# Third LayerNorm of a decoder layer: normalised by ScalarE in two passes instead of by VectorE in one

## The reference, cut to what matters

```
def _layernorm(x, axis=-1, eps=1e-05):
    m = jnp.mean(x, axis=axis, keepdims=True)
    v = jnp.var(x, axis=axis, keepdims=True)
    return (x - m) / jnp.sqrt(v + eps)
...
x = _layernorm(x + attention(x))      # 16 heads, causal, top-32 keys of each row kept
x = _layernorm(x + experts(x, ...))   # 8 experts 256 -> 512 -> 256, relu, gated sum
x = _layernorm(x + ffn(x))            # Hadamard, 4-bit activations, ternary weight
return x
```

## Time and profile before

| | |
|---|---|
| time, median of 3 runs | 606.18 us (605.2 to 607.4) |
| time of the profiled execution | 605.08 us |
| its span, first to last instruction | 603.3 us |
| busy share of the span: PE, PEld | 87%, 75% |
| busy share: DVE, ACT, POOL | 78%, 64%, 57% |
| third LayerNorm on DVE (line 841, out_sb) | 16 instructions, 9.9 us busy in all |

### The profile page before, as it was taken

One profiled execution on the slowest core, in us unless ns is written; L12 is line 12 of the kernel. 1 busy time (PEld: TensorE's weight loads), 2 busy tenths in 40 slices (PEclk: granted clock), 3 DMA queues, 4 the chain that ended last, 5 costly groups with the idle time before them and its releaser, 6 DMA issues. The chain is left out here.

```text
span 603.3 us, 22386 instructions
## 1 busy us (share of the span) xinstructions
PE 527.5 (87%) x8180; PEld 450.2 (75%) x8180; DVE 472.6 (78%) x2995; ACT 385.9 (64%) x909; POOL 344.5 (57%) x336
## 2 busy tenths in 40 slices
PE   4567459999899999998999989998999999989941
PEld 3455347888778878887888878887888888878830
DVE  1777996968988998698899998999899999633213
ACT  2787765866667667675677657776686767555520
POOL 3447661875566646555375646665656556656831
PEclk9799767999999999999999999999999999999985
DMA  7253341010000010000100100010001000000000
GB/s 217 80 184 131 109 145 37 14 37 20 3 21 20 3 54 21 2 3 3 54 20 3 56 3 20 3 55 2 20 3 38 3 3 2 20 0 3 19 0 17
DMA packets 21933, 21.85 MB, mean 36 GB/s; under 512 B 1856, under 2 KB 19776, under 8 KB 21824
## 3 DMA queue, kind: packets, MB, share of 16 engines
q1 hardware_dynamic: 21824, 20.42, 10.8%
HBM read 18.32 MB, written 2.10 MB: 34 GB/s over the span
## 5 line engine op out<-in xcount | busy, mean ns | idle before, releaser
L478 POOL TENSOR_TENSOR h_lo<-h_raw,h_hi 128x512 f16<-128x512 f32 x128 | 148.7, 1164 | 126.8 <-ACT h_raw L598 125.8
L792 PE MATMUL ps_o<-w_hi,h_lo 128*128 128x256 f16 x512 | 139.8, 273 | 4.7 <-POOL h_lo L478 4.5
L776 PE MATMUL ps_z<-x1t_hi,w_lo 128*128 128x256 f16 x512 | 140.4, 274 | 0.7 <-DVE x1t_lo L934 0.7
L776 PE MATMUL ps_z<-x1t_lo,w_hi 128*128 128x256 f16 x512 | 140.2, 274 | 0.0
L776 PE MATMUL ps_z<-x1t_hi,w_hi 128*128 128x256 f16 x512 | 140.1, 274 | 0.0
L792 PE MATMUL ps_o<-w_lo,h_hi 128*128 128x256 f16 x512 | 139.6, 273 | 0.0
L792 PE MATMUL ps_o<-w_hi,h_hi 128*128 128x256 f16 x512 | 139.6, 273 | 0.0
L878 DVE MATCH_REPLACE8 taken<-next,taken 128x48 f32<-128x48 f32 (+2 forms) x576 | 127.4, 232 | 0.1
L594 ACT ACTIVATE h_hi<-ps_z 128x512 f16<-128x512 f32 x128 | 76.0, 594 | 70.5 <-PE ps_z L776 70.4
L499 POOL TENSOR_TENSOR acc<-go_sb,acc 128x512 f32<-128x512 f32 x56 | 71.4, 1276 | 58.9 <-ACT go_sb L608 58.1
L873 DVE MAX8 next<-taken 128x8 f32<-128x48 f32 (+2 forms) x576 | 95.7, 233 | 0.0
(11 more groups left out here) (110 smaller groups left out, 950.3 us busy)
## 6 DMA issues: line engine op xcount, KB each, us to landing
w_raw<-in_w1t SPq DMA_DIRECT2D x8, 512.0 KB, 4.4
w_raw<-in_w2t SPq DMA_DIRECT2D x8, 512.0 KB, 5.5
xt_sb<-in_xt SPq DMA_DIRECT2D x8, 256.0 KB, 3.2
x_sb<-in_x SPq DMA_DIRECT2D x8, 256.0 KB, 2.9
out<-out_sb SPq DMA_DIRECT2D x8, 256.0 KB, 2.2
xa_sb<-in_xt SPq DMA_DIRECT2D x7, 256.0 KB, 3.1
ctx_sb<-in_ctx_w SPq DMA_DIRECT2D x8, 128.0 KB, 2.9
itok_sb<-in_itok SPq DMA_DIRECT2D x8, 128.0 KB, 3.0
```

What stands on the lines that cost most here:

```text
L478: nc.gpsimd.tensor_tensor(h_lo[:, e % 2, 2 * z:2 * z + 2, :], h_raw[:, z, :, :], h_hi[:, e % 2, 2 * z:2 * z + 2, :], ALU.subtract)\
L776: last = pe.matmul(ps_z[z][:, d * UT:(d + 1) * UT], w[:, e, c, at:at + P], x[:, c, :], start=n == 0, stop=n == len(terms) - 1)
L792: last = pe.matmul(ps_o[e % 2][:, b * D:(b + 1) * D], h[:, e % 2, c, b * SEQ:(b + 1) * SEQ], w[:, e, c, :], start=n == 0, stop=n == len(te ...
```

## The change

The third LayerNorm's last step goes from DVE to ACT for units 0 to 6; unit 7 keeps it on DVE. The slot stays the same, so on ACT the step stands where the slot puts it among ACT's steps:

- units 0, 2, 3, 4, 5: behind the `relu` of expert 6 of a later unit, right ahead of `copy_ot` of unit v+2;
- unit 1: between `copy_probs` of unit 4 and the last `gate_out` of unit 2;
- unit 6: between `gate_out` of expert 5 and `relu` of expert 7 of unit 7.

On ACT it takes four instructions instead of two: a pass that adds minus the mean (`Identity` with a bias operand) on both sequences, a wait until these are complete, and a pass that multiplies by rstd (`Copy` with a scale operand), in place. POOL computes minus the mean in one more 128x2 instruction inside `rstd3`, in all eight units, and its power instruction waits for both. The store's wait is unchanged.

```
-    ("pool", "rstd3"), ("dve", "ln3_apply"), ("sp", "store"),
+    ("pool", "rstd3"), ("act", "ln3_apply"), ("sp", "store"),
...
-                put(base + at[name], engine, name, v)
+                put(base + at[name], "dve" if name == "ln3_apply" and v == UNITS - 1 else engine, name, v)
...
+        minus_mean = sb("minus_mean", [P, 3, UB])
...
+        centred = [sem(f"centred{i}") for i in range(3)]
...
+                    if i == 2:
+                        nc.gpsimd.tensor_scalar(minus_mean[:, i, :], meanvar[:, i, :, 0], -1.0, None, ALU.mult)\
+                            .then_inc(eps_added[i], 1)
-                    pool.wait_ge(eps_added[i], v + 1)
+                    pool.wait_ge(eps_added[i], (2 if i == 2 else 1) * (v + 1))
...
+            def layernorm_apply(i, dst, src, v, ready):
+                act.wait_ge(rstd_ready[i], v + 1)
+                for b in range(UB):
+                    last = act.activation(dst[:, b, :], src[:, b, :], ACT.Identity, bias=minus_mean[:, i, b:b + 1])
+                last.then_inc(centred[i], 1)
+                act.wait_ge(centred[i], v + 1)
+                for b in range(UB):
+                    last = act.activation(dst[:, b, :], dst[:, b, :], ACT.Copy, scale=rstd[:, i, b:b + 1])
+                last.then_inc(ready, 1)
...
+                elif name == "ln3_apply":
+                    act.wait_ge(s_store, 16 * (v + 1))
+                    layernorm_apply(2, out_sb, t3, v, out_ready)
```

## The result

The changed kernel took 608.92 us in the median (606.96 to 610.8, 11 runs), the kernel before 606.56 us in the same session (604.1 to 607.6, 11 runs). The ratio is 1.0042 with a 95% interval of 1.0027 to 1.0056, that is 1.6 to 3.4 us more. The change makes the kernel slower, by a little under half a per cent; 608.9 us was predicted.

The account below looks back on a forecast made before the run. The prediction took the steady phase to be bound by TensorE plus a few waits per unit. Terms 3.0 + 0.05 - 0.4 + 0.1 = +2.75 us on 606.18 us gave 608.9 us, with an 8-in-10 range of 606.6 to 611.2 us.

Parts of the forecast that it names:

- units 0, 2, 3, 4: Step ahead of copy_ot delays it, so TensorE's out_proj waits 0.75 us per unit, 3.0 us in all (2.5 to 5.1).
- unit 5: Longer ScalarE idle time ahead of copy_ot: it comes 0.23 us late, mostly swallowed before out_proj; +0.05 us (0 to 0.6).
- unit 1: VectorE's relief removes TensorE's 0.39 us wait for ln2's application; gate_out's delay costs nothing; -0.4 us (0 to -0.4).
- unit 6: The relu behind the step comes 1.16 us late; the second relu's 1.53 us of idle time takes it up; 0.
- tail: Unit 7's power waits for two small POOL instructions, where everything counts; +0.1 us (0 to 0.22).
- What bounds the kernel: Steady phase bound by TensorE, which waits only 7.1 us for LayerNorms and 1.3 us for softmax weights (200 to 580 us).
- That nothing gives it back: TensorE's 1.46 us wait for turn_x1 also hangs on out_proj, so everything moves by 0.75 us and the wait stays.
- point (3): Sign expected in the profile after: TensorE's waits for turn_x1 still about 1.46 us.
- The relief that reaches TensorE: Rival: VectorE's backlog sets line 906's start, so ln1 chains come earlier; 4.0 us less, 602.1 us; chance 0.08.
- The smaller loss by half-hidden delays: Rival: copy_ot delays half hidden, 0.35 us of stall for 4 units; +1.1 us, 607.3 us; chance 0.22.
- The larger loss: Rival: ScalarE instructions or the wait between passes cost the high end, unit 5 stalling too; +5.9 us, 612.1 us; chance 0.10.

Follow-up runs that it names:

- the one pass: Changed kernel with one ScalarE instruction per sequence instead of two, same place, GpSimd multiplying minus mean by rstd; 606.44 us, ratio 1.0010 to the kernel before.
- the kernel with the step in a gap: Changed kernel with the steps of units 0, 2, 3, 4 and 5 placed behind a later relu where ScalarE idles; 604.25 us, ratio 0.9980 to the kernel before.
- relief only: Kernel before, with VectorE's third LayerNorm step of units 0 to 6 cut to one column, nothing added on ScalarE; 605.10 us, ratio 0.9990.
- delay only: Kernel before, real step kept on VectorE, four unread ScalarE instructions added at the moved step's place in units 0, 2, 3, 4, 5; 610.46 us, ratio 1.0071.
- GpSimd's instruction only: Kernel before, no step moved, GpSimd still computing the unread minus mean in all eight units; 606.08 us, ratio 0.9993.
- unit 1 alone: Kernel before with only unit 1's third LayerNorm step moved to ScalarE, with its one GpSimd instruction; 605.56 us, ratio 0.9981.

## Why the prediction was right, point by point

The predicted 608.9 us met the median of 608.92 us, but the sum behind it was too small in the profile: +2.75 us against +3.5. The difference of the medians, 2.4 us in the first session and 3.8 us in the second, lies on both sides of either. The forecast also stood on 606.18 us, the median of three runs; on the 606.56 us of the session the same sum gives 609.3 us. A base too low by 0.4 us and a difference that came out at 2.4 us in that session made up the 608.92; that the time was met to the hundredth part is luck. The terms:

| term | predicted | measured in the distance |
|---|---|---|
| units 0, 2, 3, 4 | 4 x 0.75 = 3.0 | 4 x 0.90 = 3.6 |
| unit 5 | +0.05 | +0.3 |
| unit 1 | -0.4 | -0.6 |
| unit 6 | 0 | 0 |
| tail | +0.1 | +0.3 |
| unit 3's ln1 chain | not seen | -0.2 |
| two small shifts between units 4 and 5 | not seen | +0.1 |
| sum | +2.75 | +3.5 |

**What bounds the kernel: one group of waits overlooked.** The prediction says that outside the waits for a LayerNorm and for the softmax weights TensorE runs without a gap. The same list of the kernel before, 200 to 580 us, has a third group between these two:

```profile
PE ps_o L792 <- POOL h_lo L478: 4.2, 8, 1.1
```

It did no harm: the changed kernel has the same 4.2 us in 8 places.

**The four stalls: mechanism right, size low by 0.15 us each.** The instructions took 505 and 500 ns where 0.50 us was taken between 0.47 and 0.63. The groups of ScalarE after:

```profile
L536 ACT ACTIVATE out_sb<-out_sb,rstd 128x256 f32<-128x256 f32 x14 | 6.3, 500 | 0.2
L532 ACT ACTIVATE out_sb<-t,minus_mean 128x256 f32<-128x256 f32 x14 | 6.3, 505 | 0.1
```

The Trainium skill, ScalarE: Activation LUTs, "What ACT_TABLE_LOAD costs", gives 280 ns plus 0.833 ns a column for an instruction with one pointer operand, and 93 ns for a second. The estimates from it are 493 ns here and 586 ns for the one pass; the trace agrees within 3%, with 505, 500 and 596 ns. From the step to copy_ot it took 343.51 - 341.76 = 1.75 us, predicted 1.73. Two things were missed behind it. TensorE started 0.14 us after copy_ot's end (344.33 to 344.47), not 0.05: the row that gave 0.05 was of a product with a 17-column operand and 32 columns of weights. The size of the weights doesn't explain it, since their load itself began 0.11 us after copy_ot's end:

```profile
344.44 1.59 PEld L689 LDWEIGHTS ps_misc<-wo_sb,ot_sb 128*128 128x128 f32 x8 [0.92 <-ACT ot_sb L598]
```

What does stays open. And the eight products, started after a break, took 1.97 us instead of the 1.89 they take right behind another product: +0.08. 0.83 + 0.08 = 0.9 us, and 4 x 0.9 = 3.6. The profile lists only 0.66 us of wait for a delay of 0.83 us: the last product ahead of it started at 343.53 and out_proj at 344.47, 0.94 us, where 0.10 us lay between them before (341.61 to 341.71). Products start every 0.11 us but are recorded as 0.27 us long, and a listed wait begins only at the recorded end.

**That nothing gives it back** held: the wait for turn_x1 stayed 1.45 us, as point (3) of the forecast's signs had it, and the addition's idle time rose by 1.54 us (predicted 1.5).

**Unit 5** was the step with the largest miss in proportion. Its rows after:

```profile
523.89 0.22 POOL L514 TENSOR_SCALAR minus_mean<-meanvar 128x2 f32<-128x2 f32 x1
524.20 0.71 POOL L517 TENSOR_TENSOR rstd<-var_eps,minus_half 128x2 f32<-128x2 f32 x1
525.00 0.91 ACT L532 ACTIVATE out_sb<-t,minus_mean 128x256 f32<-128x256 f32 x2
...
526.76 0.81 ACT L598 ACTIVATE ot_sb<-ps_misc,bv_sb 128x256 f32<-128x256 f32 x2
527.72 1.97 PE L689 MATMUL ps_misc<-wo_sb,ot_sb 128*128 128x256 f32 x8
```

I charged GpSimd's extra instruction with its busy time, 0.22 us; but the power starts 0.31 us after it does (523.89 to 524.20), since the wait between two dependent instructions counts too. ScalarE then started 0.09 us after rstd. Together copy_ot came 0.40 us late against TensorE's own progress instead of 0.23, which no longer fits into the 0.26 us ahead of out_proj: 0.25 us and the 0.08 us of the longer products. The bound for this term, 0.6, held.

Ahead of it lie two shifts that have nothing to do with copy_ot. From turn_x2 at 484.92 to the turn of the softmax weights at 500.20 it took 15.28 us before and 15.44 us after (489.47 to 504.91), and just as long, 15.44 us, in the kernel with the step in a gap, where copy_ot isn't late. The 11.90 us ahead of 484.92 became 11.82 us in both. Together that is +0.1 us; the cause stays open.

**Unit 1** gave back what it should and a little more. The turn_x2 behind its step, which is unit 2's, after, against its start at 299.79 with a wait of 0.39 us:

```profile
300.05 0.82 DVE L905 SCALAR_TENSOR_TENSOR p_sb<-taken,ps_s 128x640 f32<-128x640 f32 x1 [0.50 <-ACT ps_s L578]
...
301.77 0.60 PE L697 MATMUL ps_misc<-ident,x 128*128 128x128 f32 x4
```

Now keep waits for exp, as written, and TensorE runs on. The gain is 0.55 us where 0.39 us of wait were listed, for the reason given under the stalls: before, turn_x2 started 0.66 us after the start of the last product ahead of it (299.13), now 0.11 us (301.66). The prediction took the listed wait for the cost.

**Unit 6** went as worked out: the relu behind the step came 1.17 us late (predicted 1.16) and the second relu took it up, so TensorE lost nothing.

**The tail**: +0.3 us instead of +0.1, and above its bound of 0.22. Its rows after:

```profile
603.87 0.22 POOL L511 TENSOR_SCALAR var_eps<-meanvar 128x2 f32<-128x2 f32 x1 [1.38 <-DVE meanvar L852]
604.17 0.22 POOL L514 TENSOR_SCALAR minus_mean<-meanvar 128x2 f32<-128x2 f32 x1
604.48 0.71 POOL L517 TENSOR_TENSOR rstd<-var_eps,minus_half 128x2 f32<-128x2 f32 x1
```

The power started 0.61 us after var_eps; before, it was 0.30 us. The instruction costs the distance of two starts. The term went wrong as in unit 5: a busy time was taken for the price of a link in a chain. Unit 7 doesn't even use the result.

**Not foreseen**, -0.2 us: in unit 3, a group of eight MAX8 (the first maxima of a selection) on VectorE ahead of ln1's application took 1.42 us before and 1.18 us after. The first row is of the kernel before, the second of the one after:

```profile
282.65 1.42 DVE L853 MAX8 top<-s_sb 128x8 f32<-128x16 f32 x8
```

```profile
285.39 1.18 DVE L871 MAX8 top<-s_sb 128x8 f32<-128x16 f32 x8
```

The instructions themselves are no slower, 176 to 273 ns each before and 177 to 276 ns after; before, VectorE stood still between the second and the third. The stretch around it (us, length, busy us and instructions of PE, PEld, DVE, ACT, POOL, granted clock, DMA share, GB/s) has it busy for 0.06 of 0.20 us:

```profile
282.90:283.10 0.20, 0.20 (x4) 0.18 (x3) 0.06 (x2) 0.00 (x0) 0.20 (x1) 1.00 0.00 0
```

The wait for turn_x1 behind it was 1.66 us before and 1.45 us after, which is the "1.7" of the earlier trace rows. The longer group is at this place in all kernels in which VectorE's instructions up to there are those of the kernel before (before, relief only, delay only, GpSimd's instruction only, and unit 1 alone, whose step comes later), and in none of those that take unit 0's step from VectorE (1.18 us in all of them). So it goes with VectorE's instruction stream, not with what ScalarE and GpSimd do; the break of 0.20 us in the kernel with unit 1 alone looks like another of the kind. What in the stream makes them wasn't tried and stays open.

**The rivals.** The relief that reaches TensorE is refuted where it was priced: with relief alone the 0.28 us became idle time, and in the changed kernel so did the full 0.73 us. The smaller loss by half-hidden delays, too: none of the four was hidden. The larger loss is the side on which the terms erred, but its cause was another: the instructions and the wait between the passes came at the value taken, not at the high end.

## What to carry to other kernels

Before a step is moved to an engine because that engine is less busy, look at what stands behind it in that engine's queue: the same four instructions cost 0.9 us a unit ahead of a copy that TensorE waits for, and nothing behind a relu a few microseconds later. Price a small instruction in a dependent chain by the distance of two starts (0.31 us here), not by its busy time (0.22 us), and count a new wait of TensorE with the slower start behind it, and from start to start: the listed waits of 0.66 us were 0.83 us of delay. Taking load from a busy engine is worth its time only where the profile shows that the step ahead of a wait had no idle time before it, as in one of seven units here.

## What the runs showed of the hardware that I had not expected

- Eight 128x256 f32 products took 1.97 us when they started after a break (0.66 us listed, or, with one pass, too short to be listed) and 1.89 us right behind others; and the first started 0.14 us after the end of the ScalarE instruction that it waited for.
- TensorE's listed waits fall short of the delay: 0.66 us listed for 0.83 us, 0.39 for 0.55, 2.40 for 2.56.
- Waits of 0.66 us left TensorE's granted clock at 1.00 (216 to 220, 344 to 348, 408 to 412 and 472 to 476 us of the changed kernel). Two waits of 2.40 us were followed by a fall to the lower level, with out_proj at 2.95 and 3.44 us instead of 1.97; two others of the same length were not. What tells them apart stays open.
- A group of eight MAX8 took 1.42 us instead of 1.18 us at one place of the program, kernel after kernel, until VectorE's instructions ahead of it changed: not by slower instructions, but by a break between two of them with nothing that it waited for.
